# Gate's three products of a chunk, then up's three; gated rows' buffers 320 bytes further on

## What is computed

```python
x = x + xattn(layernorm(x), ctx, wq, wk, wv, wo)      # keys: 4096 context rows and 256 new ones
x = x + mla(layernorm(x), Wqa, Wqb, Wkva, Wkvb, Wo)   # 16 heads, causal, rotary parts
x = x + moe(layernorm(x), router, w_gate, w_up, w_down, shared weights)
```

```python
gate = jax.lax.ragged_dot(xs, w_gate, group_sizes)     # 512 -> 256 per expert
up   = jax.lax.ragged_dot(xs, w_up, group_sizes)
down = jax.lax.ragged_dot(jax.nn.silu(gate) * up, w_down, group_sizes)   # 256 -> 512
routed = (down[unsort].reshape(T, K, H) * tkw[..., None]).sum(axis=1)
```

## Time and profile before

| | us |
|---|---|
| timed executions | 521.10, 524.14, 527.57 |
| profiled execution | 521.37 |
| its span, from the first to the last instruction | 519.6 |
| PE busy in the span | 507.4 |
| DVE busy | 402.2 |
| ACT busy | 302.3 |
| routed experts in column form, first matmul to the end | from 249.92 |

### The profile page before, as it was taken

One profiled execution on the slowest core, in us unless ns is written; L12 is line 12 of the kernel. 1 busy time (PEld: TensorE's weight loads), 2 busy tenths in 40 slices (PEclk: granted clock), 3 DMA queues, 4 the chain that ended last, 5 costly groups with the idle time before them and its releaser, 6 DMA issues.

```text
span 519.6 us, 10261 instructions
## 1 busy us (share of the span) xinstructions
PE 507.4 (98%) x3798; PEld 471.0 (91%) x3798; DVE 402.2 (77%) x627; ACT 302.3 (58%) x437; POOL 29.5 (6%) x49
## 2 busy tenths in 40 slices
PE   8999999999999999989999999999999999999997
PEld 7999989999778998969899999999999999999997
DVE  6777668987888887877797768677776877778675
ACT  5656457773367677665654665646555465655631
POOL 1000000000623113001000000000000000000000
PEclk9999999999999999999999999999999999999999
DMA  8765543663412233424536565554646556564521
GB/s 285 302 215 190 188 137 110 185 211 118 151 37 78 77 120 123 133 111 167 195 127 209 165 228 160 207 193 170 226 153 227 175 189 202 168 232 154 212 71 40
DMA packets 19460, 86.25 MB, mean 166 GB/s; under 512 B 2160, under 2 KB 2416, under 8 KB 19312
## 3 DMA queue, kind: packets, MB, share of 16 engines
q1 hardware_dynamic: 19440, 85.99, 49.1%
HBM read 85.46 MB, written 0.52 MB: 165 GB/s over the span
## 4 chain that ended last, share of the span: by engine, by line
PE 85%; DVE 9%; ACT 3%; issue 2%; DMA 1%; ACTq 0%; DVEq 0%
PE bank L1013 32%; PE bank L443 13%; PE bank L447 12%; PE bank L446 12%; PE bank L451 4%; PE bank L454 4%; PE bank L455 4%; DVE w_lo L296 2%; PE bank L792 1%; ACT w_hi L291 1%; PE bank L812 1%; DVE score_rows L1411 1%; DVE operands L1416 1%; PE bank L773 1%; DMA first_rows<-x_dram 1%
## 5 line engine op out<-in xcount | busy, mean ns | idle before, releaser
L291 ACT CAST w_hi<-raw 128x768 fp32r<-128x768 f32 (+3 forms) x158 | 160.0, 1043 | 97.7 <-PE bank L1013 82.5
L296 DVE TENSOR_TENSOR w_lo<-raw,w_hi 128x1280 fp32r<-128x1280 f32 (+3 forms) x156 | 183.3, 1213 | 15.4 <-ACT w_hi L291 14.2
L1013 PE MATMUL bank<-xt_hi,w_lo 128*128 128x256 f32 x512 | 105.3, 277 | 0.0
L1013 PE MATMUL bank<-xt_hi,w_hi 128*128 128x256 f32 x512 | 105.3, 277 | 0.0
L1013 PE MATMUL bank<-xt_lo,w_hi 128*128 128x256 f32 x512 | 105.1, 277 | 0.0
L1013 PEld LDWEIGHTS bank<-xt_hi,w_hi 128*128 128x128 f32 x512 | 81.8, 188 | 2.7
L1013 PEld LDWEIGHTS bank<-xt_lo,w_hi 128*128 128x128 f32 x512 | 79.8, 188 | 0.0
L1013 PEld LDWEIGHTS bank<-xt_hi,w_lo 128*128 128x128 f32 x512 | 79.7, 188 | 0.0
L443 PE MATMUL bank<-w_hi,operands 128*128 128x512 f32 (+1 forms) x194 | 75.0, 387 | 1.5 <-DVE operands L344 1.0
L447 PE MATMUL bank<-w_hi,operands 128*128 128x512 f32 (+1 forms) x194 | 74.1, 382 | 0.0
L446 PE MATMUL bank<-w_lo,operands 128*128 128x512 f32 (+1 forms) x194 | 73.8, 380 | 0.0
(11 more groups left out here) (202 smaller groups left out, 864.5 us busy)
## 6 DMA issues: line engine op xcount, KB each, us to landing
raw<-w_exp_dram SPq DMA_DIRECT2D x34, 896.0 KB, 4.7
raw<-w_exp_dram SPq DMA_DIRECT2D x34, 640.0 KB, 5.6
raw<-ctx_t_dram SPq DMA_DIRECT2D x16, 512.0 KB, 4.9
raw<-ctx_n_dram SPq DMA_DIRECT2D x16, 512.0 KB, 4.3
raw<-w_mla_dram SPq DMA_DIRECT2D x8, 512.0 KB, 3.6
raw<-w_mla_dram SPq DMA_DIRECT2D x8, 448.0 KB, 3.7
raw<-wq_dram SPq DMA_DIRECT2D x4, 256.0 KB, 5.3
raw<-wk_dram SPq DMA_DIRECT2D x2, 512.0 KB, 7.3
```

Of the source, the lines that this page charges most:

```text
L291: act.copy(w_hi[:, t.slot, at:at + n], raw[:, t.slot, at:at + n]).then_inc(hi_split[k], 1)
L296: eng.tensor_tensor(w_lo[:, t.slot, at:at + n], raw[:, t.slot, at:at + n], w_hi[:, t.slot, at:at + n].bitcast(F32), ALU.subtract) \
L1013: return pe.matmul(bank[b + u][:, m * T:m * T + T], a[:, t.slot, at + m * P:at + m * P + P], x[:, c, :], start=c == 0 and a is w_hi and x ...
```

## The change

In `gate_up` the loop over gate and up is now outside the one over the three products: for each half and chunk, gate's three matmuls come one after the other, then up's three. Before, the two took turns product by product, except in the last chunk of the second half, which had them apart already. The three products also come in another order: high x high, weights high x tokens low, weights low x tokens high, so that two matmuls in a row load the same block. `used[0]` is told at the middle one of up's last three. The views `h_hi` and `h_lo` begin 80 words, which is 320 bytes, further on in `operands`; their sizes and their distance from each other are the same.

```diff
--- before.py
+++ after.py
@@ -187,7 +187,7 @@
         qr_hi, qr_lo = mpt_hi[:, :, 384:512], mpt_lo[:, :, 384:512]
         mo_hi, mo_lo = op(6656, 2, T), op(11264, 2, T)
 
-        h_hi, h_lo = op(0, 2, 512), op(1024, 2, 512)
+        h_hi, h_lo = op(80, 2, 512), op(1104, 2, 512)
 
 
         score_rows = sb("score_rows", [P, 2 * KEYS])
@@ -1012,27 +1012,22 @@
                     at = (u * NC + c) * I if k == 0 else OFF[2] + (c - 1) * I
                     return pe.matmul(bank[b + u][:, m * T:m * T + T], a[:, t.slot, at + m * P:at + m * P + P],
                                      x[:, c, :], start=c == 0 and a is w_hi and x is xt_hi,
-                                     stop=c == NC - 1 and x is xt_lo)
+                                     stop=c == NC - 1 and a is w_lo)
 
                 for m in range(2):
                     for c in range(NC):
                         if m == 0 and c < 2:
                             ready(t, 2 * c)
-                        products = ((w_hi, xt_hi), (w_lo, xt_hi), (w_hi, xt_lo))
-                        if m == 1 and c == NC - 1:
-                            for u in range(2):
-                                for a, x in products:
-                                    ins = gate_or_up(u, m, c, a, x)
-                                    if u == 1 and a is w_lo:
-                                        ins.then_inc(used[0], 1)
-                                ins.then_inc(bank_full[b + u], 1)
-                        else:
-                            for a, x in products:
-                                ins = gate_or_up(0, m, c, a, x)
+                        for u in range(2):
+                            for a, x in ((w_hi, xt_hi), (w_hi, xt_lo), (w_lo, xt_hi)):
+                                ins = gate_or_up(u, m, c, a, x)
                                 if told is not None:
                                     ins.then_inc(told, 1)
                                     told = None
-                                gate_or_up(1, m, c, a, x)
+                                if m == u == 1 and c == NC - 1 and a is w_hi and x is xt_lo:
+                                    ins.then_inc(used[0], 1)
+                            if m == 1 and c == NC - 1:
+                                ins.then_inc(bank_full[b + u], 1)
 
             def down(j, s, told=None):
```

## The result

The changed kernel takes 527.35 us (median of 22 runs, 525.69 to 530.40), the kernel before in the same comparison 525.55 us (22 runs, 520.89 to 529.26): a ratio of 1.0059, 95% interval 1.0032 to 1.0086. That is within 2%, but it is slower, where 522.0 us were forecast. The two sets differ in shape too. The runs of before lie in two groups, eleven from 520.9 to 524.1 and eleven from 527.0 to 529.3, with nothing between; those of the changed kernel form one group. What that means is only seen in the experiments.

What follows compares the result with a forecast made beforehand. PE, 85% of the chain and busy 507.4 of 519.6 us, was taken as the bound, so only matmul pace counts. Profiled 521.4 + 0 + 0, set towards the runs' middle 522.8, gave 522.0 us, range 518.6 to 528.4.

Steps and rivals of the forecast that it cites:

- the order costs nothing by itself: In `gate_up`: the new product order adds 0, since the score groups already run this sequence at 276 ns.
- no wait, release or queue moved: Around `gate_up`: banks and `used[0]` are told at the same matmuls, other engines keep their order; cost 0.
- the two paces of 276 and 281 ns: 256-column matmul records come in two lengths; a stretch keeps one, and the slow pace costs 5 ns a matmul, 4%.
- the slow pace holds through every `gate_up`: Rival: every `gate_up` stays slow throughout, 521.4 + 6.5 = 527.9 us; chance 0.22.
- What may move is the pace at which an expert enters: At the start of each `gate_up`, under the new order: -1.1 us at best, +6.5 at worst, taken as 0.
- entered from the same `down` 29 times in a row with the same result: Reason given for taking 0 for the entry of `gate_up`, from its own rows in the earlier trace.
- The address was costed only inside `down`'s own 12 matmuls: Buffers 320 bytes further on: -1.3 us at best, +4.4 at worst over 33 experts, taken as 0.
- the bound of the entry: Worst case for `gate_up` staying slow throughout: 0.21 us in each of 31 experts, +6.5 us.
- the rival with 530.5 us: Every `gate_up` slow and every `down` following at 398 ns, 2.6 us on top of 527.9; within the 0.22 chance.
- The single wait of the earlier trace: From 260 to 505 us, holding 29 experts, PE waited for another engine once, for 0.6 us.
- the sum: Whole kernel: profiled 521.4 us plus 0 for the order and 0 for the address leaves 521.4.
- The rule of two independent ports: Weight loads take no read bandwidth from the running matmul, so order and address could not matter: 521.4 us without a range.

Runs made afterwards that it cites:

- the run of the distances: Kernel before plus 96 stretches of matmuls alone behind its end, streamed block moved 16 bytes between stretches; total time tells nothing, starts lay 113.3 to 120.0 ns apart with 256 columns.
- The lone matmuls: Stretches of matmuls appended behind the kernel before, one weight block reloaded for each, only the streamed block's start moved, ACT and DVE done; 113.3 ns a start at 64 bytes, 120.0 at 0.

## Why the prediction was wrong

*What held.* The bound (PE without waits, so pace alone counts); the order costs nothing by itself; no wait, release or queue moved; the two paces of 276 and 281 ns; and the size of "the slow pace holds through every `gate_up`": 0.21 us an expert was its price, 0.187 came, and its 527.9 us stands beside 527.35. That nearness is partly luck: of the 5.7 us above before's lower group the experts make up 30 x (8.373 - 8.213) = 4.8, and the rival left out `down`, which gave 0.8 back; what fills the rest is not shown for the timed runs (in the profiled one it was the later start of the experts, 1.5, with the score groups slow).

*The step that failed* is "What may move is the pace at which an expert enters", costed under the order of the products and taken as 0 because `gate_up` had been "entered from the same `down` 29 times in a row with the same result". The changed `down` is not the same `down` to the matmul that follows: its loads begin elsewhere, and that decides how `gate_up` is entered. The address was costed only inside `down`'s own 12 matmuls, between -1.3 and +4.4 us; there it gave -0.8, within the bound and with the other sign than the loss. It should have carried the bound of the entry too, +6.5 us. The 29 equal entries were one observation: a cycle that keeps itself up gives 29 equal rows whichever cycle it is in. The rival had a chance of 0.22, hung on the order; hung on the address, with two paces seen in the very same lines, it would have deserved more.

*What was in view.* The earlier trace rows showed `gate_up` in its slow pace in the kernel before. The `down` that follows at 398 in the earlier trace rows is not that of the slow cycle, as the rival with 530.5 us took it to be: it took 2.800 us, the `gate_up` behind it came out quick, and in the slow cycle `down` takes 2.767, with 391 to 394 on its lines. And the three timed runs, 521.10, 524.14 and 527.57, were read as scatter around one value. By the groups the first two belong to one cycle and the third to the other, 6.2 us apart, which the run of the distances shows at 8.420 against 8.213 us. The single wait of the earlier trace rows was passed over too: it stands where the two cycles part. So the sum rested on the quick cycle (521.4, profiled), and the median it was measured against is a mixture: 525.55, 522.66, 523.78 and 521.79 us in four comparisons. The change removes the quick cycle and leaves a slow one that is 30 x (8.420 - 8.373) = 1.4 us better; against before's lower group it costs 527.35 - 521.65 = 5.7 us, 1.1%, and against the upper one it gains 1.3.

*The rule weighed there.* The lone matmuls show 113.3 and 120.0 ns a start for the same load beside the same stream, with only the start of the stream moved. The rule of two independent ports, from the Trainium skill's "TensorE: Matmul & The Clock Gate", section "Step-by-step: what each phase is for", would have both equal. Here the measurement decides against it for what a load costs the stream beside it; the number of ports is not shown by any run.

*Left open.* What in the reads repeats after 256 bytes, and what in the 0.6 us wait at 264 us, or in the `down` behind it, puts an execution of the kernel before into one cycle or the other; no run separates causes for either. The share of runs in the upper group differed much between the comparisons (11 of 22, 8 of 23, 5 of 11, 1 of 29).

## What to carry to other kernels

Where matmuls follow one another without a wait, read the step from start to start and compare it over stretches: two values for one instruction can mean that the place of the loaded block against the streamed one matters, and then an edit of an address is an edit of the pace, of that stage and of the one behind it. Equal rows of a loop are one observation, not as many as there are rows, when each pass begins in the state that the last one left; timed runs in two groups can be the sign of two such states. Before a pace is tuned by moving a tile, choose a distance that returns to the quick pace by itself, and look up the address that the allocation really gave.

## What the runs showed of the hardware

- A 256-column matmul of this type, with a weight load beside it, starts 113.3 ns after the one before it at best, and 115.6 to 129.0 on average at most distances of the two blocks modulo 256 bytes; 4 bytes can make the difference (144: 113.3 at the end of the stretch; 148: 120.0; 152: 130.0). The granted clock was 1.00 throughout, the level of 2.4 GHz.
- At 64 bytes two paces, 113.3 and 117.7, both last; at 144 the slow start dies out within eight to fourteen matmuls; at nearly all the others the stretch settles into a repeating pattern of slow steps.
- 512-column matmuls have such paces too: `down` took 2.720 us for 12 with its loaded block moved by 64 or 320 bytes, 2.747 and 2.767 (and once in each trace 2.800) at 0, 2.775 at 192, and 2.79 to 2.80 at 128 and 384.
- The state outlives a change of tile, of width and of bank: it is handed from `gate_up` to `down` and back, through 30 experts.
